# A fused attention and feed-forward kernel on one core: gate peaks taken from signed integers, all gate integers formed on ScalarE, forty of 48 gate units finished in the up pass and ten kept on chip

## The chip, the cores and the metric

The kernel runs on one core of a Trainium2 chip. The metric is device time of one execution in microseconds, as the median of several executions.

## The reference

Only the second half of the reference is touched by the change. With `x` of 8192 tokens by 512, and weights of 512 by 1536, it is

```python
def act_qdq(x):                      # 16 bits, one scale for the whole tensor
    scale = jnp.maximum(jnp.max(jnp.abs(x)) / qmax, 1e-12)
    return jnp.clip(jnp.round(x / scale), -qmax - 1.0, qmax) * scale

x = act_qdq(layernorm(x))
up = act_qdq(x @ lpbq_dequant(w_up).T)
gate = act_qdq(x @ lpbq_dequant(w_gate).T)
sig = fixed_qdq_u16(jax.nn.sigmoid(gate))     # round to 1/65536
gate = act_qdq(gate * sig)
o = act_qdq(gate * up)
return o @ lpbq_dequant(w_down).T             # added to the residual
```

Each `act_qdq` needs the largest magnitude of a whole tensor before its first integer can be formed. So there are four points at which everything waits for a peak: after `gate`, after `gate * sig`, after `up`, and after `gate * up`.

## The kernel before

The tokens are cut into 16 blocks of 512, and the 1536 columns into three parts of 512. One block by one part is a unit, 128 partitions by 2048 elements; there are 48 of each of `gate`, `up` and the product. After an attention part (the first 620 us), `feed` runs four stages.

**Gate pass.** TensorE makes the 48 gate units (L1778), each as two pairs of 1024 columns in four PSUM buffers. ScalarE copies each pair out (`evict`, L1640), VectorE takes the largest magnitude of the unit (`raw_peak`, L1421), and GpSimd's queue stores the raw float unit to DRAM. The raw unit sits in one of three buffers. Between these, the up and down weights are quantised: VectorE forms values (L1448, L1450), ScalarE their high halves (L1650).

**Up pass.** TensorE makes the 48 up units in the same way. Beside it, the other engines work on `gate`, in the order of a loop over the 48 tiles `n`. `first(u)` comes seven times in four tiles, from tile 0 to 26: the raw unit is loaded back into one of four buffers `gin`, made into 16-bit integers in a ring of four (on ScalarE, L1662, for every third unit, on VectorE, L1493, for the others) and stored; ScalarE also forms the magnitude of the integers in `ab` (L1664) and the sigmoid (L1666); VectorE rounds the sigmoid to an integer (`sigmoid_integer`, L1498) and multiplies magnitude and sigmoid with a running maximum (L1505). After all 48 the peak of `gate * sig` is known, and `second(v)`, two per tile from tile `SECOND` on, finishes `READY` units: sigmoid again (L1674), rounded (L1498), multiplied and scaled to the integers of the gated value (L1511), which go to DRAM and, for the first `KEPT` units, also stay in SBUF. For 13 of them (`DONE`: the kept ones and five late ones) ScalarE takes the magnitude in place right there (`magnitude`, L1682).

**Between the passes.** TensorE has nothing to do until the peak of `gate * up` is known. A loop over the 48 units, in an order made up beforehand, multiplies the magnitude of the gated integers with the magnitude of the up integers on VectorE, with a running maximum (`prod`, L1576). ScalarE forms the up magnitudes (`ua`, L1721) from raw up units that are loaded again; seven buffers hold them, so that a load is issued when the unit seven places before it is used. The gated integers are loaded by GpSimd's queue up to seven places ahead (`NEAR`), into `WQ` slots and into those of resident units that are used up. How a unit's gated magnitude comes about is its `made`:

- `done`: the magnitude is there, nothing is left to do
- `act`: ScalarE takes it (L1725)
- `dve`: VectorE takes it (L1567 and L1569)
- `late`: the unit was not finished in the up pass. ScalarE forms the sigmoid (L1708), VectorE rounds it (L1498) and multiplies (L1560), ScalarE scales and takes the magnitude (L1728)

The late units are spread evenly over the loop. With 36 finished units, the 48 are 12 late, 13 done, 15 act and 8 dve.

**Down pass.** With the peak known, the product's integers are formed unit by unit and TensorE multiplies them with the down weights (L1792).

Each engine runs its own list in order, with semaphores between them.

Of the kernel before, what the change touches and what calls it, by code (L numbers as in the profile page):

```python
# [6 lines left out]
F32 = mybir.dt.float32  # L7
F16 = mybir.dt.float16
I16 = mybir.dt.int16
U16 = mybir.dt.uint16  # L10
# [24 lines left out]
UN = 4  # L35
UNITS = FC // UN
UE = UN * BLK
READY = 36
EARLY = 4
XR = 9  # L40
KEPT = 8


def need(eng, sem, value):
# [868 lines left out]
def feed_memory(s, keep):  # L913

    for n, shape in (("up", [P, 2, DC, F]), ("down", [P, 2, FC, D])):
        keep[n + "_all"] = s.sb(n, shape, F16)
        keep[n] = [keep[n + "_all"][:, i] for i in range(2)]
    mem = {"gin": s.sb("gin", [P, 4, UE], F32), "ring": s.sb("ring", [P, 4, UE], I16),
           "sig": s.sb("sig", [P, 3, UE], F32), "sq": s.sb("sq", [P, UE], U16),
           "ab": s.sb("ab", [P, 2, UE], I16), "hq": s.sb("hq", [P, 2, DC * BLK], I16),  # L920
           "h_parts": s.sb("h_parts", [P, 2, 2, SUB, DC, P], F16), "raw": s.sb("raw", [P, UNITS, UE], F32)}
    for n in ("red_w", "all_w", "unit_w", *(f"{a}_{b}" for a in "gpuo" for b in ("red", "all"))):
        mem[n] = s.sb(n, [P, 1], F32)
    return mem


def feed(nc, keep, mem, hT_d, hq_d, gate_d, up_d, gate_q, x1_d, out, NB, scale_d, mats):
# [16 lines left out]
    SECOND = NU - READY // 2  # L944
    DONE = list(range(KEPT)) + [v for v in range(KEPT, READY) if v - KEPT >= AGAIN - AR][:5]
    LOADED = AGAIN - AR
    WQ, NEAR = 4, 7
    FG, FU = 4, 3
    hT_v = hT_d.rearrange("(b n) p d -> b p n d", n=SUB)
    out_v = out.rearrange("(b n p) d -> b p n d", p=P, n=SUB)  # L950
# [51 lines left out]
    with Scope(nc, "fd") as s:  # L1002
# [14 lines left out]
        def floats(t):  # L1017
# [23 lines left out]
                  for n in ("gate_all", "up_all"))  # L1041
# [16 lines left out]
        x_in, y_out = [s.sem(f"x_in{i}") for i in range(2)], [s.sem(f"y_out{i}") for i in range(2)]  # L1058
        m = s.sems("g_red g_all p_red p_all u_red u_all o_red o_all dve g_scales u_scales o_scales "
                   "hq ah al mm out peak w_peak w_red w_all w_scales w_sent w_q w_real w_hi w_lo "  # L1060
                   "gq_act gq_dve ab sig sq gpeak g2 mag gp neg ga_late ga_act ga_dve ua prod "
                   "fsig fsq fgp fgq fuq fo foq foh fol fmm y")
        gpk, gpk_v, gpk_p = whole_peak(nc, mem, m, "g", keep["gate_peak"][:, :])
        ppk, ppk_v, ppk_p = whole_peak(nc, mem, m, "p", keep["gated_peak"][:, :])
        upk, upk_v, upk_p = whole_peak(nc, mem, m, "u", keep["up_peak"][:, :])
        opk, opk_v, opk_p = whole_peak(nc, mem, m, "o", keep["o_peak"][:, :])
# [21 lines left out]

        def kept(j):

            return spare[:, j, :] if j < 6 else more[:, j - 6, :]

        def integers(u):

# [12 lines left out]

        def have_gq(eng, u):

            if u % 3 == 0:  # L1110
                eng.wait_ge(m["gq_act"], u // 3 + 1)
            else:
                eng.wait_ge(m["gq_dve"], u - u // 3)

        def gq_free(eng, u):

            if QR <= u < AWAY:
                eng.wait_ge(gq_out[u % QR], 16 * (u // QR))
                eng.wait_ge(m["sig"], u - QR + 1)

        def sig_free(eng, k):

# [17 lines left out]
        def gated(i):  # L1140

            kind, j = g_slot[i][0] if home[i] == "load" else ("unit", order[i])
            if kind == "wq":
                return hq[:, j, :] if j < 2 else ab[:, j - 2, :]
            return again(j - AWAY if j >= AWAY else j + KEPT)

        def have_gated(eng, i):
# [34 lines left out]
        with nc.Block() as block:  # L1182
            @block.sync
            def _(sp):
# [30 lines left out]
                def load_gate(u):  # L1215
                    if u < NU:
                        if u < GR:
                            sp.wait_ge(m["w_lo"], 2 * PIECES)
                            sp.wait_ge(m["hq"], NB)
                            sp.wait_ge(stored[u % UNITS], 16 * (u // UNITS + 1))  # L1220
                        else:
                            have_gq(sp, u - GR)
                            sp.wait_ge(m["ab"], u - GR + 1)
                            sp.wait_ge(stored[u % UNITS], 16 * (u // UNITS + 1))
                        sp.dma_start(gin[:, u % GR, :], gate_d[u // UNITS, u % UNITS]).then_inc(gate_in[u % GR], 16)

                def load_again(w):
                    if w < AGAIN:
                        if w < AR:
                            sp.wait_ge(m["sig"], NU)  # L1230
                            sp.wait_ge(m["ab"], NU)
                            for r in range(QR):
                                sp.wait_ge(gq_out[r], 16 * stored_first(r))
                        else:
                            sp.wait_ge(again_out[w % AR], 16 * (w // AR))
                        sp.dma_start(again(KEPT + w), gate_q[w]).then_inc(again_in[w % AR], 16)
# [90 lines left out]
            def _(pool):  # L1327
# [34 lines left out]
                for n in range(NU):  # L1362
# [5 lines left out]
                    if k == 1:  # L1368
                        pool.wait_ge(m["w_red"], i + 1)
                        nc.gpsimd.partition_all_reduce(allm[:, :], red[:, :], P, PEAK).then_inc(m["w_all"], 1)  # L1370
                gpk_p(pool)
                for n in range(NU):
                    if n == SECOND:
                        ppk_p(pool)
# [29 lines left out]
            def _(dve):  # L1404
# [13 lines left out]
                def raw_peak(n):  # L1418
                    dve.wait_ge(m["out"], 2 * n + 2)
                    to, k = ("gate_peak", n) if n < NU else ("up_peak", n - NU)  # L1420
                    nc.vector.tensor_reduce(keep[to][:, k:k + 1], raw[:, n % UNITS, :], AX.X, ALU.max,  # L1421
                                            apply_absolute_value=True).then_inc(m["peak"], 1)

# [52 lines left out]
                            weight_low(i, k // 2 - 3)  # L1476

                dve.wait_ge(m["peak"], NU)
                gpk_v(dve)
                link(nc.vector.tensor_tensor(g[:, 3:4], g[:, 0:1], al_[:, 5:6], ALU.mult))  # L1480
                dve.wait_ge(m["g_all"], 1)
                quantiser(nc, link, g[:, 4:5], g[:, 5:6], gpk[:, :], g[:, 2:3])
                nc.vector.tensor_scalar(g[:, 6:7], g[:, 4:5], 1.0 / 65536.0, None, ALU.mult).then_inc(m["g_scales"], 1)
                dve.wait_ge(m["g_scales"], 1)
                dve.wait_ge(m["w_lo"], 2 * PIECES)

                def gate_integers(u):
                    if 0 <= u < NU and u % 3:
                        dve.wait_ge(gate_in[u % GR], 16 * (u // GR + 1))
                        gq_free(dve, u)  # L1490
                        if u >= AWAY:
                            dve.wait_ge(m["mm"], NB * PAIRS)
                        nc.vector.tensor_scalar(integers(u), gin[:, u % GR, :], g[:, 5:6], None, ALU.mult).then_inc(m["gq_dve"], 1)  # L1493

                def sigmoid_integer(k, a):
                    dve.wait_ge(m["sig"], k + 1)
# [3 lines left out]

                def first(u):
                    sigmoid_integer(u, u % 2)
                    gate_integers(u + 2)
                    dve.wait_ge(m["ab"], u + 1)
                    nc.vector.tensor_tensor_reduce(out=sig[:, u % 2, :], in0=ab[:, u % 2, :], in1=sq[:, :], scale=1.0,  # L1505
                                                   scalar=0.0, op0=ALU.mult, op1=ALU.max,
                                                   accum_out=keep["gated_peak"][:, u:u + 1]).then_inc(m["gpeak"], 1)

# [2 lines left out]
                    nc.vector.scalar_tensor_tensor(out=again(v), in0=sq[:, :], scalar=g[:, 7:8], in1=again(v),  # L1511
                                                   op0=ALU.mult, op1=ALU.mult).then_inc(m["g2"], 1)

                gate_integers(1)
                for n in range(NU):
                    if n % UNITS == 1 and n // UNITS + 1 < NB:
                        split(NB + n // UNITS + 1)
                    for u in first_units(n):
                        first(u)
                    if n == SECOND - 1:  # L1520
                        dve.wait_ge(m["gpeak"], NU)
                        ppk_v(dve)
                    if n == SECOND:
                        dve.wait_ge(m["p_all"], 1)
                        quantiser(nc, link, g[:, 8:9], g[:, 7:8], ppk[:, :], g[:, 6:7])
                    for v in second_units(n)[:1]:
                        second(v)
                    raw_peak(NU + n)
                    for v in second_units(n)[1:]:
                        second(v)  # L1530
# [97 lines left out]
            def _(act):  # L1628
# [24 lines left out]
                    evict(n, 0)  # L1653
                    evict(n, 1)

                def first(u):
                    act.wait_ge(gate_in[u % GR], 16 * (u // GR + 1))
                    if u % 3 == 0:
                        gq_free(act, u)
                        if u >= AWAY:  # L1660
                            act.wait_ge(m["mm"], NB * PAIRS)
                        nc.scalar.activation(integers(u), gin[:, u % GR, :], ACT.Copy, scale=g[:, 5:6]).then_inc(m["gq_act"], 1)  # L1662
                    need(act, m["gpeak"], u - 1)
                    nc.scalar.activation(ab[:, u % 2, :], gin[:, u % GR, :], ACT.Abs, scale=g[:, 5:6]).then_inc(m["ab"], 1)  # L1664
                    have_gq(act, u)
                    nc.scalar.activation(sig[:, u % 2, :], integers(u), ACT.Sigmoid, scale=g[:, 4:5]).then_inc(m["sig"], 1)  # L1666

# [16 lines left out]
                act.wait_ge(m["g_scales"], 1)  # L1684
                act.wait_ge(m["w_lo"], 2 * PIECES)
                act.wait_ge(m["hq"], NB)
                for n in range(NU):
                    for u in first_units(n)[:1]:
                        first(u)
                    for v in second_units(n)[:1]:  # L1690
# [107 lines left out]
def build(nc, x, ctx_t, idx_t, wq_t, wkv_t, wo_t, gate_n, up_n, up_t, down_n, down_t, out, B, LKV):  # L1798
# [13 lines left out]
    with Scope(nc, "kept") as s:  # L1812
# [2 lines left out]

            "g": s.sb("g", [P, 16], F32),
            "h_peak": s.sb("h_peak", [P, NT // 2], F32), "gate_peak": s.sb("gate_peak", [P, U3], F32),
            "up_peak": s.sb("up_peak", [P, U3], F32), "gated_peak": s.sb("gated_peak", [P, U3], F32),
            "o_peak": s.sb("o_peak", [P, U3], F32),
        }  # L1820
        with Scope(nc, "kept") as s_gate:
# [62 lines left out]
```

## Time and profile before

| | us |
|---|---|
| median of 3 runs (2324.28 to 2326.08) | 2325.39 |
| the profiled execution | 2322.58 |
| its span, first to last instruction | 2320.7 |

The rows below are of the profiled execution; times are microseconds from the start of its span. PE is TensorE, DVE VectorE, ACT ScalarE, POOL GpSimd, SP the queue of loads. L1576 is line 1576 of the kernel before.

### The profile page before, as it was taken

To read this page: it belongs to the slowest core of one execution; us is meant where nothing else is said; L and a number is where in the kernel's file an instruction comes from. 1 tells how busy PE (TensorE), PEld (TensorE's weight loads), DVE (VectorE), ACT (ScalarE), POOL (GpSimd) and SP (SyncE) were. 2 spreads that over 40 slices of the span, in tenths; PEclk is the share of its full clock that TensorE was granted. 3 is DMA by queue.
4 is the path that set the end of the run, shared out by engine and by line. 5 is a ranking of instruction groups with operands and counts; after the bars stand their busy time and mean duration, and the time that the engine had idled before them with its cause. 6 is when DMAs were issued, how large, how long until landed. Compare 5 with 4: busy or idle time off the path is not lost.

```text
span 2320.7 us, 25770 instructions
## 1 busy us (share of the span) xinstructions
PE 2031.3 (88%) x9780; PEld 975.5 (42%) x9780; DVE 1678.2 (72%) x1385; ACT 1401.9 (60%) x1599; POOL 578.9 (25%) x600
## 2 busy tenths in 40 slices
PE   5899999998699999999999999998000799999998
PEld 2455555554344444444444444444000344444443
DVE  8799999999444443532699997999899644488641
ACT  4588888886322322322698995666899643467530
POOL 2587777776100000000112111222110000000000
PEclk9999999999799999999999999999555899999999
DMA  7689999997348647633899994787998755545641
GB/s 294 261 312 364 361 366 364 355 371 300 136 167 267 258 164 230 223 144 141 299 393 382 376 363 176 295 322 288 414 417 328 284 227 216 205 195 218 236 154 73
DMA packets 131163, 634.63 MB, mean 273 GB/s; under 512 B 12256, under 2 KB 12768, under 8 KB 91104
## 3 DMA queue, kind: packets, MB, share of 16 engines
q1 hardware_dynamic: 85888, 316.81, 37.3%
q0 software_dynamic: 45152, 316.16, 34.8%
q8 instruction: 78, 1.28, 0.2%
q14 instruction: 45, 0.37, 0.0%
HBM read 430.69 MB, written 202.24 MB: 273 GB/s over the span
## 4 chain that ended last, share of the span: by engine, by line
PE 64%; DVE 3%; issue 3%; ACT 2%; POOL 0%; DVEq 0%; ACTq 0%; POOLq 0%
PE fd_pp L1778 43%; PE fd_pp L1792 21%; ACT ff_ring L1721 1%; DVE ff_sig L1576 1%; DVE ff_h_parts L1560 1%; DVE ff_sq L1498 1%; ACT ff_sig L1708 0%; DVE ff_sq L1567 0%; DVE kept_gate L1569 0%; DVE ff_gin L1511 0%; DVE ff_hq L1550 0%; ACT ff_ring L1747 0%; ACT ff_sig L1737 0%; ACT ff_hq L1633 0%; DVE kept_o_peak L1576 0%
## 5 line engine op out<-in xcount | busy, mean ns | idle before, releaser
L1792 PE MATMUL fd_pp<-ff_down,kept_gate 128*128 128x512 f16 x1536 | 457.9, 380 | 193.1 <-DVE ff_up L1617 193.1
L1778 PE MATMUL fd_pp<-ff_h_parts,kept_gate 128*128 128x512 f16 x2304 | 500.4, 381 | 14.7 <-DVE ff_h_parts L1416 14.7
L1778 PE MATMUL fd_pp<-ff_h_parts,ff_up 128*128 128x512 f16 x2304 | 497.4, 379 | 0.0
L1640 ACT ACTIVATE ff_raw<-fd_pp 128x1024 f32<-128x1024 f32 x192 | 194.3, 1017 | 397.4 <-PE fd_pp L1778 397.4
L1778 PEld LDWEIGHTS fd_pp<-ff_h_parts,kept_gate 128*128 128x128 f16 x2304 | 226.1, 98 | 288.8 <-DVE ff_h_parts L1416 15.0
L1778 PEld LDWEIGHTS fd_pp<-ff_h_parts,ff_up 128*128 128x128 f16 x2304 | 225.4, 98 | 271.8
L1421 DVE TENSOR_REDUCE kept_gate_peak<-ff_raw 128x1 f32<-128x2048 f32 x48 | 109.7, 2285 | 293.5 <-ACT ff_raw L1640 293.5
L1792 PEld LDWEIGHTS fd_pp<-ff_down,kept_gate 128*128 128x128 f16 x1536 | 150.4, 98 | 375.2 <-issue 194.7
L1792 PE MATMUL fd_pp<-ff_down,ff_up 128*128 128x512 f16 x768 | 291.6, 380 | 0.0
L1747 ACT ACTIVATE ff_ring<-ff_hq,kept_g 128x2048 int16<-128x2048 f32 x48 | 96.0, 1999 | 189.5 <-DVE ff_hq L1550 188.2
L787 PE MATMUL at_psO<-kept_wo,at_ahi 128*128 128x512 f16 x512 | 154.9, 384 | 15.9 <-ACT at_alo L278 10.1
L1615 DVE CAST kept_gate<-ff_ring 128x2048 f16<-128x2048 int16 x48 | 33.3, 693 | 178.5 <-PE fd_pp L1792 135.1
L787 PE MATMUL at_psQ<-kept_wq,at_xhi 128*128 128x512 f16 x512 | 156.2, 387 | 1.4 <-ACT at_xlo L269 1.4
L518 DVE TENSOR_TENSOR at_kv_rows<-at_kv_rows,at_psQ 128x2048 f32<-128x2048 f32 x64 | 144.2, 2280 | 9.0 <-DMA at_kv_rows<-kv_table,kept_rows 5.0
L696 POOL TENSOR_TENSOR at_kv_rows<-at_kv_rows 128x1024 f32<-128x1024 f32 x62 | 146.7, 2367 | 4.9
L523 DVE TENSOR_REDUCE at_sc<-at_kv_rows 128x64 f32<-128x2048 f32 x64 | 142.9, 2274 | 0.0
L689 POOL TENSOR_TENSOR at_kv_rows<-at_kv_rows,at_pr 128x1024 f32<-128x1024 f32 x64 | 123.5, 1930 | 78.0 <-DVE at_kv_rows L528 74.2
L1335 POOL DMA_DIRECT2D gate_scratch<-ff_raw x48 | 26.5, 553 | 464.1 <-DVE kept_gate_peak L1421 464.1
L1395 POOL DMA_DIRECT2D out<-ff_h_parts x15 | 12.5, 834 | 466.0 <-DVE ff_h_parts L1593 439.0
L1498 DVE TENSOR_SCALAR ff_sq<-ff_sig 128x2048 uint16<-128x2048 f32 x96 | 117.3, 1222 | 9.5 <-ACT ff_sig L1666 6.0
L1421 DVE TENSOR_REDUCE kept_up_peak<-ff_raw 128x1 f32<-128x2048 f32 x48 | 109.5, 2282 | 18.5 <-ACT ff_raw L1640 18.2
L1792 PEld LDWEIGHTS fd_pp<-ff_down,ff_up 128*128 128x128 f16 x768 | 75.3, 98 | 91.1 <-issue 0.8
(239 smaller groups left out, 3311.8 us busy)
## 6 DMA issues: line engine op xcount, KB each, us to landing
ff_raw<-up_scratch SPq DMA_DIRECT2D x66, 1024.0 KB, 8.5
gate_scratch<-ff_raw POOLq DMA_DIRECT2D x48, 1024.0 KB, 9.1
ff_gin<-gate_scratch SPq DMA_DIRECT2D x48, 1024.0 KB, 8.4
up_scratch<-ff_raw POOLq DMA_DIRECT2D x48, 1024.0 KB, 6.8
ff_gin<-gate_integers SPq DMA_DIRECT2D x73, 512.0 KB, 6.3
gate_integers<-ff_ring POOLq DMA_DIRECT2D x43, 512.0 KB, 8.7
ff_up<-up_scratch SPq DMA_DIRECT2D x21, 1024.0 KB, 9.1
kept_xs<-in_x SPq DMA_DIRECT2D x32, 512.0 KB, 12.3
```

The source lines that it names most:

```text
L518: nc.vector.tensor_tensor(keys, keys, psQ[t % 2][:, :].unsqueeze(1).to_broadcast([P, W, D]), ALU.mult).then_inc(m["prod"], 1)
L523: nc.vector.tensor_reduce(raw[:, t % 2], kv[:, t % KR, :, 0:D].rearrange("p w (h e) -> p w h e", h=H), AX.X, ALU.add).then_inc(m["raw"], 1)
L689: nc.gpsimd.tensor_tensor(upper, upper, pr[:, t % 2, 2:4].unsqueeze(3).to_broadcast([P, 2, H, HD]), ALU.mult).then_inc(m["last"], 1)
L696: nc.gpsimd.tensor_tensor(lower, lower, upper, ALU.add).then_inc(m["half"], 1)
L787: mm = nc.tensor.matmul(out[:, :], a[:, slot, c, :], w[b][:, c, :], start=(q == 0), stop=(q == len(todo) - 1))
L1421: nc.vector.tensor_reduce(keep[to][:, k:k + 1], raw[:, n % UNITS, :], AX.X, ALU.max, apply_absolute_value=True).then_inc(m["peak"], 1)
L1498: nc.vector.tensor_scalar(sq[:, :], sig[:, a, :], 65536.0, 65535.0, ALU.mult, ALU.min).then_inc(m["sq"], 1)
L1615: nc.vector.tensor_copy(piece(oh, k), fo_oq).then_inc(m["foh"], 1)
L1640: nc.scalar.activation(raw[:, n % UNITS, h * 2 * BLK:(h + 1) * 2 * BLK], pp[(2 * n + h) % 4][:, :, :].rearrange("p a t -> p (a t)"), ACT.C ...
L1747: nc.scalar.activation(fo_oq, fo_o, ACT.Copy, scale=g[:, 13:14]).then_inc(m["foq"], 1)
L1778: mm = nc.tensor.matmul(pp[k % 4][:, h, :], wt[w][:, c, f:f + P], a[:, b % 2, :, c, :], start=(q == 0), stop=(q == len(todo) - 1))
L1792: mm = nc.tensor.matmul(pp[k % 8 // 2][:, k % 2, :], a[b % 2][:, f, t * P:(t + 1) * P], wt[w][:, f, :], start=(q == 0 and i == 0), stop=(q ...
```

## The change

The product's peak is now made from the signed gate integers: their product with the sigmoid, times -1, gives the largest negative one, and the largest positive one is worked out from the largest gate value alone (a second reduction, without magnitude, per unit of the gate pass), since the gated value grows with a positive gate. The magnitudes in `ab` are gone, and its two buffers keep two more finished units; ScalarE forms the integers of all 48 units, one unit ahead of its sigmoid. `READY` goes from 36 to 40, so that `SECOND` goes from tile 30 to 28, `KEPT` from 8 to 10, and `WQ` from 4 to 2.

```diff
-READY = 36
+READY = 40
...
-KEPT = 8
+KEPT = 10
...
-    WQ, NEAR = 4, 7
+    WQ, NEAR = 2, 7
...
-            return spare[:, j, :] if j < 6 else more[:, j - 6, :]
+            return spare[:, j, :] if j < 6 else more[:, j - 6, :] if j < 8 else ab[:, j - 8, :]
...
-            if u % 3 == 0:
-                eng.wait_ge(m["gq_act"], u // 3 + 1)
-            else:
-                eng.wait_ge(m["gq_dve"], u - u // 3)
+            eng.wait_ge(m["gq"], u + 1)
...
             if QR <= u < AWAY:
                 eng.wait_ge(gq_out[u % QR], 16 * (u // QR))
-                eng.wait_ge(m["sig"], u - QR + 1)
+                eng.wait_ge(m["gpeak"], u - QR + 1)
...
                             have_gq(sp, u - GR)
-                            sp.wait_ge(m["ab"], u - GR + 1)
...
-                gpk_p(pool)
+                pool.wait_ge(m["g_red"], 1)
+                nc.gpsimd.partition_all_reduce(g_all[:, :], g_red[:, :], P, PEAK).then_inc(m["g_all"], 1)
...
+                    if n < NU:
+                        nc.vector.tensor_reduce(keep["gate_top"][:, n:n + 1], raw[:, n % UNITS, :], AX.X, ALU.max)
                     nc.vector.tensor_reduce(keep[to][:, k:k + 1], raw[:, n % UNITS, :], AX.X, ALU.max,
                                             apply_absolute_value=True).then_inc(m["peak"], 1)
...
-                gpk_v(dve)
+                nc.vector.tensor_reduce(g_red[:, 0:1], keep["gate_peak"][:, :], AX.X, ALU.max)
+                nc.vector.tensor_reduce(g_red[:, 1:2], keep["gate_top"][:, :], AX.X, ALU.max).then_inc(m["g_red"], 1)
...
+                nc.vector.tensor_scalar(top_i[:, :], g_all[:, 1:2], g[:, 5:6], None, ALU.mult).then_inc(m["top"], 1)
+
+                def greatest_gated():
+                    dve.wait_ge(m["top_s"], 1)
+                    nc.vector.tensor_scalar(top_q[:, :], top_s[:, :], 65536.0, 65535.0, ALU.mult, ALU.min).then_inc(m["top_q"], 1)
+                    dve.wait_ge(m["top_q"], 1)
+                    link(nc.vector.tensor_tensor(keep["gated_peak"][:, NU:NU + 1], top_i[:, :], top_q[:, :], ALU.mult))
...
                 def first(u):
                     sigmoid_integer(u, u % 2)
-                    gate_integers(u + 2)
-                    dve.wait_ge(m["ab"], u + 1)
-                    nc.vector.tensor_tensor_reduce(out=sig[:, u % 2, :], in0=ab[:, u % 2, :], in1=sq[:, :], scale=1.0,
+                    nc.vector.tensor_tensor_reduce(out=sig[:, u % 2, :], in0=integers(u), in1=sq[:, :], scale=-1.0,
...
+                    if n == 2:
+                        greatest_gated()
...
-                def first(u):
-                    act.wait_ge(gate_in[u % GR], 16 * (u // GR + 1))
-                    if u % 3 == 0:
+                def gate_integers(u):
+                    if u < NU:
+                        act.wait_ge(gate_in[u % GR], 16 * (u // GR + 1))
                         gq_free(act, u)
                         if u >= AWAY:
                             act.wait_ge(m["mm"], NB * PAIRS)
-                        nc.scalar.activation(integers(u), gin[:, u % GR, :], ACT.Copy, scale=g[:, 5:6]).then_inc(m["gq_act"], 1)
+                        nc.scalar.activation(integers(u), gin[:, u % GR, :], ACT.Copy, scale=g[:, 5:6]).then_inc(m["gq"], 1)
+
+                def first(u):
+                    gate_integers(u + 1)
                     need(act, m["gpeak"], u - 1)
-                    nc.scalar.activation(ab[:, u % 2, :], gin[:, u % GR, :], ACT.Abs, scale=g[:, 5:6]).then_inc(m["ab"], 1)
                     have_gq(act, u)
                     nc.scalar.activation(sig[:, u % 2, :], integers(u), ACT.Sigmoid, scale=g[:, 4:5]).then_inc(m["sig"], 1)
...
+                gate_integers(0)
                 for n in range(NU):
+                    if n == 1:
+                        act.wait_ge(m["top"], 1)
+                        nc.scalar.activation(top_s[:, :], top_i[:, :], ACT.Sigmoid, scale=g[:, 4:5]).then_inc(m["top_s"], 1)
```

## Rows read from the trace of the kernel before

**Rows 1.** TensorE's waits: what waited for what, us in total, times, longest.

```profile
PE fd_pp L1792 <- DVE ff_up L1617: 193.1, 1, 193.1
```

**Rows 2.** Stretches: length, busy us of five engines, clock, DMA share, GB/s.

```profile
620.00:1120.80 500.80, 499.97 (x2303) 226.06 (x2304) 196.13 (x120) 135.06 (x118) 34.52 (x64) 0.99 0.58 203
1120.80:1618.50 497.70, 497.67 (x2306) 225.44 (x2304) 464.27 (x336) 395.39 (x256) 97.24 (x126) 1.00 0.84 321
...
1627.50:1802.10 174.60, 0.00 (x0) 0.00 (x0) 163.30 (x138) 162.77 (x86) 17.38 (x28) 0.50 0.94 384
1640.00:1740.00 100.00, 0.00 (x0) 0.00 (x0) 95.04 (x79) 96.27 (x52) 10.81 (x18) 0.50 1.02 419
1121.00:1411.00 290.00, 290.00 (x1345) 131.52 (x1344) 277.50 (x224) 265.55 (x168) 51.16 (x68) 1.00 0.91 349
```

**Rows 3.** Timeline between the passes: start, length, engine, line, operation, idle before.

```profile
1623.08 2.00 ACT L1708 ACTIVATE ff_sig<-ff_hq,kept_g 128x2048 f32<-128x2048 int16 x1
...
1627.59 5.79 ACT L1721 ACTIVATE ff_ring<-ff_raw,kept_g 128x2048 int16<-128x2048 f32 x3 [2.51 <-DVE kept_g L1536]
...
1781.82 1.89 ACT L1725 ACTIVATE ff_ab<-ff_ab 128x2048 int16<-128x2048 int16 x1
...
1783.62 1.99 ACT L1708 ACTIVATE ff_sig<-ff_sig,kept_g 128x2048 f32<-128x2048 int16 x1
...
1785.51 1.98 ACT L1721 ACTIVATE ff_ring<-ff_raw,kept_g 128x2048 int16<-128x2048 f32 x1
...
1789.75 1.22 DVE L1498 TENSOR_SCALAR ff_sq<-ff_sig 128x2048 uint16<-128x2048 f32 x1
...
1791.00 2.29 DVE L1560 TENSOR_TENSOR ff_h_parts<-ff_sig,ff_sq 128x2048 f32<-128x2048 int16 x1
1793.33 2.00 ACT L1728 ACTIVATE ff_sig<-ff_h_parts,kept_g 128x2048 int16<-128x2048 f32 x1 [0.25 <-DVE ff_h_parts L1560]
1793.43 0.69 DVE L1567 TENSOR_SCALAR ff_sq<-ff_gin 128x2048 int16<-128x2048 int16 x1
...
1795.30 2.29 DVE L1576 CUSTOM_DVE_ANT_0 ff_sig<-kept_gate,ff_ring 128x2048 bf16<-128x2048 int16 x1
...
1797.51 2.29 DVE L1576 CUSTOM_DVE_ANT_0 ff_sig<-ff_gin,ff_ring 128x2048 bf16<-128x2048 int16 x1
...
1801.94 0.08 DVE L1576 DVE_READ_ACCUMULATOR2_ANT kept_o_peak<- 128x1 f32 x1
```

**Rows 4.** Waits of VectorE and ScalarE between the passes, the longest that repeat.

```profile
DVE ff_sig L1576 <- ACT ff_ring L1721: 9.9, 9, 2.2
...
ACT ff_hq L1728 <- DVE ff_h_parts L1560: 2.6, 3, 2.1
```

**Rows 5.** Loads issued from 1618, 1630 and 1720 us on: size, us to landing.

```profile
ff_hq<-gate_integers POOLq DMA_DIRECT2D x1, 512.0 KB, 12.1
...
ff_up<-up_scratch SPq DMA_DIRECT2D x2, 1024.0 KB, 12.4
...
ff_raw<-up_scratch SPq DMA_DIRECT2D x3, 1024.0 KB, 6.9
```

**Rows 6.** Groups of instructions of the up pass: count, busy us, mean ns.

```profile
L1493 DVE TENSOR_SCALAR ff_ring<-ff_gin,kept_g 128x2048 int16<-128x2048 f32 x26 | 33.4, 1286 | 0.9
...
L1662 ACT ACTIVATE ff_ring<-ff_gin,kept_g 128x2048 int16<-128x2048 f32 x14 | 27.9, 1994 | 4.6 <-DVE kept_g L1483 4.6
```

**Rows 7.** Timeline from the gate pass to the up pass.

```profile
1121.03 44.19 PE L1778 MATMUL fd_pp<-ff_h_parts,ff_up 128*128 128x512 f16 x204
...
1122.29 2.29 DVE L1421 TENSOR_REDUCE kept_gate_peak<-ff_raw 128x1 f32<-128x2048 f32 x1 [8.07 <-ACT ff_raw L1640]
...
1133.97 1.00 ACT L1640 ACTIVATE ff_raw<-fd_pp 128x1024 f32<-128x1024 f32 x1
```

**Rows 8.** The gate pass: a wait of ScalarE, and the stores with us to landing.

```profile
ACT ff_up L1650 <- DVE ff_ring L1450: 23.2, 4, 5.8
...
gate_scratch<-ff_raw POOLq DMA_DIRECT2D x47, 1024.0 KB, 9.1
```

More of the change, by code:

```diff
@@ L921, in feed_memory @@
            "h_parts": s.sb("h_parts", [P, 2, 2, SUB, DC, P], F16), "raw": s.sb("raw", [P, UNITS, UE], F32)}
-    for n in ("red_w", "all_w", "unit_w", *(f"{a}_{b}" for a in "gpuo" for b in ("red", "all"))):
+    for n in ("red_w", "all_w", "unit_w", *(f"{a}_{b}" for a in "puo" for b in ("red", "all"))):
         mem[n] = s.sb(n, [P, 1], F32)
+    for n in ("g_red", "g_all"):
+        mem[n] = s.sb(n, [P, 2], F32)
+    mem["top_i"], mem["top_s"], mem["top_q"] = (s.sb(n, [P, 1], dt) for n, dt in (("top_i", I16), ("top_s", F32), ("top_q", U16)))
     return mem
@@ L1060, in feed @@
                    "hq ah al mm out peak w_peak w_red w_all w_scales w_sent w_q w_real w_hi w_lo "
-                   "gq_act gq_dve ab sig sq gpeak g2 mag gp neg ga_late ga_act ga_dve ua prod "
+                   "gq sig sq gpeak top top_s top_q g2 mag gp neg ga_late ga_act ga_dve ua prod "
                    "fsig fsq fgp fgq fuq fo foq foh fol fmm y")
-        gpk, gpk_v, gpk_p = whole_peak(nc, mem, m, "g", keep["gate_peak"][:, :])
+        g_red, g_all, top_i, top_s, top_q = (mem[n] for n in ("g_red", "g_all", "top_i", "top_s", "top_q"))
         ppk, ppk_v, ppk_p = whole_peak(nc, mem, m, "p", keep["gated_peak"][:, :])
@@ L1143, in gated @@
             if kind == "wq":
-                return hq[:, j, :] if j < 2 else ab[:, j - 2, :]
+                return hq[:, j, :]
             return again(j - AWAY if j >= AWAY else j + KEPT)
@@ L1229, in load_again @@
                         if w < AR:
-                            sp.wait_ge(m["sig"], NU)
-                            sp.wait_ge(m["ab"], NU)
+                            sp.wait_ge(m["gq"], NU)
+                            sp.wait_ge(m["gpeak"], NU)
                             for r in range(QR):
@@ L1478, in _ @@
                 dve.wait_ge(m["peak"], NU)
-                gpk_v(dve)
+                nc.vector.tensor_reduce(g_red[:, 0:1], keep["gate_peak"][:, :], AX.X, ALU.max)
+                nc.vector.tensor_reduce(g_red[:, 1:2], keep["gate_top"][:, :], AX.X, ALU.max).then_inc(m["g_red"], 1)
                 link(nc.vector.tensor_tensor(g[:, 3:4], g[:, 0:1], al_[:, 5:6], ALU.mult))
                 dve.wait_ge(m["g_all"], 1)
-                quantiser(nc, link, g[:, 4:5], g[:, 5:6], gpk[:, :], g[:, 2:3])
+                quantiser(nc, link, g[:, 4:5], g[:, 5:6], g_all[:, 0:1], g[:, 2:3])
                 nc.vector.tensor_scalar(g[:, 6:7], g[:, 4:5], 1.0 / 65536.0, None, ALU.mult).then_inc(m["g_scales"], 1)
@@ L1485, in _ @@
                 dve.wait_ge(m["w_lo"], 2 * PIECES)
[L1487 to L1493, printed above, removed]
+                nc.vector.tensor_scalar(top_i[:, :], g_all[:, 1:2], g[:, 5:6], None, ALU.mult).then_inc(m["top"], 1)
[4 more added lines that the diff above has]
+                    link(nc.vector.tensor_tensor(keep["gated_peak"][:, NU:NU + 1], top_i[:, :], top_q[:, :], ALU.mult))
                 def sigmoid_integer(k, a):
@@ L1512, in second @@
                                                    op0=ALU.mult, op1=ALU.mult).then_inc(m["g2"], 1)
-                gate_integers(1)
                 for n in range(NU):
+                    if n == 2:
+                        greatest_gated()
                     if n % UNITS == 1 and n // UNITS + 1 < NB:
@@ L1817, in build @@
             "h_peak": s.sb("h_peak", [P, NT // 2], F32), "gate_peak": s.sb("gate_peak", [P, U3], F32),
-            "up_peak": s.sb("up_peak", [P, U3], F32), "gated_peak": s.sb("gated_peak", [P, U3], F32),
+            "up_peak": s.sb("up_peak", [P, U3], F32), "gated_peak": s.sb("gated_peak", [P, U3 + 1], F32),
+            "gate_top": s.sb("gate_top", [P, U3], F32),
             "o_peak": s.sb("o_peak", [P, U3], F32),
```

## The prediction

> **What bounds the kernel now.** I read TensorE's waits first, because three of the four stages are matrix products. After the start of the gate pass the list holds one entry: 193.1 us before the first product of the down pass [rows 1]. Nothing else in three passes of about 500 us makes TensorE wait. The stretches say the same: in the gate pass and in the up pass it is busy for all but one microsecond [rows 2]. So time can come from one place, the gap between the up pass and the down pass, and be lost in the gate and up passes, where the change lengthens other engines' lists.
>
> I then looked at what fills the gap. From the first up magnitude at 1627.59 to the last product's accumulator at 1801.94 plus 0.08 [rows 3] are 174.4 us, and in them VectorE is busy 163.30 and ScalarE 162.77 us [rows 2]: two engines share the bound, handing work to each other. What lies around these 174.4 us (the last matmul to the peak of up before, the chain over the last peak to the first product behind) is made of the same instructions in both kernels.
>
> Last I looked at the transfers, for a third bound as near: the DMA share is 1.02 at 419 GB/s from 1640 to 1740 us, and 0.94 over the whole gap [rows 2].
>
> **The gap, unit by unit.** Durations overlap at their ends, so I price an instruction by the step to the next start [rows 3]. Every unit costs ScalarE one up magnitude, 1.89 (5.79 for three in a row gives 1.90), and VectorE one product, 2.21 (1795.30 to 1797.51). A late unit adds on ScalarE 1.89 (sigmoid, 1783.62 to 1785.51) and 1.91 (its magnitude, 2.00 less the same overlap), 3.80 together; on VectorE 1.25 (1789.75 to 1791.00) and 2.21 (a 2.29 us operation less the overlap), 3.46 together. An act unit adds 1.80 on ScalarE (1781.82 to 1783.62), a dve unit 1.87 on VectorE (1793.43 to 1795.30), a done unit nothing.
>
> Going through the loop that makes the order by hand gives, with L late, d done, a act, v dve:
>
> Before: ddd, Ldad, Lvda, Ldad, Lvda, Ldad, Lvda, Ldav, four times Laav, L: 12 late, 13 done, 15 act, 8 dve.
>
> After: dddda, Ldvdad, Ladvda, Ldadvd, Ladadv, Ldaava, Lavaav, Laavaa, L: 8 late, 15 done, 17 act, 8 dve.
>
> The totals before are ScalarE 48 x 1.89 + 12 x 3.80 + 15 x 1.80 = 163.3 (161.4 without the first sigmoid, which runs at 1623.08 ahead of the stretch) and VectorE 48 x 2.21 + 12 x 3.46 + 8 x 1.87 = 162.6, against 162.77 and 163.30 measured [rows 2], so the prices hold to 1%. After, they are 151.7 and 148.8.
>
> Since the up magnitudes run only three ahead, the engines can't trade slack over long stretches. So I take for each group the greater demand. Before: 6.6 for ddd; 13.16 (ScalarE) for each of three Ldad; 14.17 (VectorE) for each of three Lvda and for Ldav; 14.96 (ScalarE) for each of four Laav; 5.7 for the last L; 168.3 together. The measured 174.4 is 6.1 more: 2.1 until the first magnitude is ready, and some 0.3 in each ScalarE group, where the engines wait for each other [rows 4]. After: 11.25, then 18.59 (VectorE), 18.74, 18.59, 18.74, 20.54, 20.54, 22.34 (ScalarE), and 5.7: 155.0, which is 13.3 less. I add 0.5 to the overhead: the first sigmoid belongs to the sixth unit now and no longer runs ahead of the stretch, and the first gated unit is wanted as the fifth unit's magnitude, at 1627.59 + 5 x 1.9 = 1637.1, while a load issued there landed 12.1 us after its issue [rows 5], about 1638.5; VectorE's rounding and product of the late unit cover most of that. **The gap shrinks by 12.8 us.**
>
> If the engines never waited for each other, ScalarE's 151.7 with 2.1 at the start and one product behind would take 156.0, 18.4 less than now. That is the bound above. For the one below see the loads.
>
> **The other parts.** *Gate pass.* 48 more reductions. The trace has no reduction without a magnitude; it may cost as little as the 0.69 of VectorE's quickest pass over a unit [rows 3], or as much as the 2.29 with one [rows 7]; I take 2.29, the same operation on the same tile. That is 106 us on VectorE at a step of 2.2, where it is busy 196.13 of 500.8 [rows 2]. What waits behind it is the store, and ScalarE for the weight pieces, now 5.8 us each (23.2 over four), then 8.0. A raw buffer is wanted again five pairs of 5.18 us (497.7 / 96) after its last copy, 25.9; reduction, store and landing take 2.3 + 0.3 + 9.1 [rows 8], then 2.2 more, which leaves 12. ScalarE late by 2.2 finds TensorE up to four pairs ahead. Cost nothing; with the cover gone, 2.2 per unit.
>
> *The seam.* The gate scale comes 2.5 us later (the second reduction of the last unit and three tiny operations). The first copy of the up pass stands behind three ScalarE operations in both versions; it ended at 1134.97 [rows 7], and TensorE needs its buffer for the fifth pair at 1120.8 + 4 x 5.18 = 1141.5. Of 6.5 us, 4.0 stay. Cost nothing. The one-column sigmoid and its integer lie between 0.08, the shortest one-column row [rows 3], and 1 us, once: nothing.
>
> *Up pass.* VectorE loses 32 gate integers (1.286 each [rows 6]) and gains four finished units of some 3.5: 464 becomes 438 of 497.7. ScalarE loses 48 magnitudes, gains 32 integers, four sigmoids and two more magnitudes in place: 395 becomes about 376. In the first 290 us, where both run fullest (277.5 and 265.6 [rows 2]), they fall to about 238 and 236. The product with scale -1 is taken at the 2.29 of the same operation in the gap [rows 3]; it could cost 40% more before VectorE were as full as now. Finishing starts at tile 28 instead of 30, and the firsts end in tile 26; with VectorE at 238 of 290 they no longer run behind their tiles, so the earlier start finds the peak known. The queues carry four more stores of finished units and two more loads of integers, and two stores of integers less, 0.524 MB each: 2.1 MB more beside the 160 of this pass (321 GB/s for 497.7 us), whose share is 0.84. TensorE was never held, so all this relief is worth nothing.
>
> The Trainium skill (ScalarE: Activation LUTs, Rules for kernel authors) advises against this move: multiplications belong on VectorE, up to about three times faster in bf16. Rows 6 agree in direction, with 1.286 against 1.994 us; the sum would be worse by that only if ScalarE were the bound of the up pass.
>
> *Down pass.* Four fewer late units are formed again, under TensorE's work: nothing. Its clock stands at 0.50, the 1.2 GHz level, in the gap while it idles [rows 2], and it starts from there either way.
>
> **The sum.** Against the profiled 2322.58 us: 2309.8. The median of the runs lies 2.8 above that execution, so I predict **2312.6**.
>
> **Rivals.** *The loads pace the gap.* 45 raw up units of 1.049 MB and 29 gated ones of 0.524 (31 less two that are loaded early) were 62.4 MB; after, 28 of the latter make it 61.9. If the stretch at share 1.02 can't shorten, it gives back 0.5 MB, 1.3 us at 419 GB/s; only the last third, where ScalarE's 16 units cost 59.8 and then 57.8, gives 2 more: **2322**. For it speaks the share. In the four groups of six that follow the first five units, 24 up and 14 gated loads are 32.5 MB, 77.6 us, against 74.7 of work. Against it speaks the time to landing, which falls from 12.4 to 6.9 us through the stage [rows 5]: the queue drains, and no engine waits for a load [rows 4]. It would now grow by some 3 us, to 15, where a load is issued seven units, 22 us, ahead.
>
> The Trainium skill (DMA: Bandwidth & Descriptors, Where 436 GB/s comes from) has a rule by which this rival would win outright: between HBM and SBUF the limit of about 358 GB/s per core binds. By it 61.9 MB take an estimated 173 us, and the gap could not shrink. Here the trace disagrees, with 419 GB/s held for 100 us.
>
> *ScalarE holds the up pass.* Each gate integer now waits in ScalarE's list, ahead of the PSUM copies, for its load and for the store of the unit four before. Seven units and eight copies need 7 x 3.8 + 8 x 1.0 = 34.6 of four tiles' 41.5 us, so 1.0 us of wait per unit is free. Beyond that TensorE falls behind; from 1.35 the gain is spent and 4.7 us more. At 2.0 per unit it costs 48: **2361**. Against it: four units are 23.7 us, and landing takes 9 to 12 [rows 5, 8]; every third unit waited so before, and TensorE did not.
>
> *The handovers eat half.* Groups of six cluster ScalarE's extra work; at 1 us of waits more per group the gain is 6: **2319**.
>
> **How the numbers follow.** The likeliest case, a gain of 10 to 16, has 0.76; handovers or loads in part, 5 to 10, have 0.10; more than 16 has 0.03; these are faster. The loads in full, or nothing for another reason, 0.06; a held up pass or gate pass, 0.05. About 0.2%, 4.7 us, is what a measurement can tell from no change. So faster 0.89, same 0.06, slower 0.05. The likeliest case alone is 2309.5 to 2315.5; the range goes from the engine bound, 2307.0, to near the handover case, 2318.5.
>
> **What would show it.** TensorE's wait ahead of the down pass at 180 instead of 193.1 us, and still no other after 621 us; eight late units; ScalarE at about 152 us of busy time there, VectorE at 149; a DMA share of 1.0 that lasts to the end of the loads, with landing at 11 to 15 us and no wait of the up magnitudes for a load. The prediction is wrong if those magnitudes wait for DMA, or if TensorE waits for a ScalarE copy in the up pass.

## The result, and the profile after

The changed kernel takes 2347.73 us in the median (2344.23 to 2350.41, 4 runs), against 2324.84 (2323.17 to 2326.08) for the kernel before: a ratio of 1.0098, interval 1.0081 to 1.0116. It is slower by 23 us, where 12.8 us of gain were forecast.

TensorE's waits, read first again, answer to [rows 1]:

```profile
PE fd_pp L1799 <- DVE ff_up L1618: 193.0, 1, 193.0
PE fd_pp L1785 <- DVE ff_h_parts L1416: 31.0, 4, 14.4
```

The wait ahead of the down pass is as long as before, and the second line is new in its count: one of its four is the 14.4 us at the start of the gate pass, which was there before too (14.73 us before the product at 620.83); the other three, 16.6 us together, lie in the up pass. L1416 is VectorE's `split` of a block's hidden integers (`hq`) into the two halves that TensorE multiplies. The chain of waits names what holds it (start, length, what; the lines of three of four such places):

```profile
1477.25 2.30 DVE kept_up_peak L1423
1480.78 5.01 DMA gate_integers<-ff_gin
1486.18 5.55 DMA ff_hq<-h_integers
...
1519.54 6.46 DMA gate_integers<-ff_gin
1526.38 4.47 DMA ff_hq<-h_integers
...
1558.68 6.17 DMA gate_integers<-ff_gin
1565.24 4.71 DMA ff_hq<-h_integers
```

A store of finished gate integers ends, and only then a load of `hq` starts. The timeline of the second place shows the engines (with the idle time before, and its releaser):

```profile
1519.54 0.53 POOL L1346 DMA_DIRECT2D gate_integers<-ff_gin  x1
...
1526.02 0.32 SPq L1235 DMA_DIRECT2D ff_gin<-gate_integers  x1
1526.38 0.54 SPq L1213 DMA_DIRECT2D ff_hq<-h_integers  x1
...
1530.88 0.69 DVE L1414 CAST ff_h_parts<-ff_hq 128x2048 f16<-128x2048 int16 x1 [9.06 <-DMA ff_hq<-h_integers]
...
1532.89 3.60 PE L1785 MATMUL fd_pp<-ff_h_parts,ff_up 128*128 128x512 f16 x9 [4.93 <-DVE ff_h_parts L1416]
...
1534.06 2.00 ACT L1677 ACTIVATE ff_sig<-ff_gin,kept_g 128x2048 f32<-128x2048 int16 x1 [9.82 <-DVE ff_sq L1500]
```

The order on SP's queue explains it. In tile `n`, SP issues the `hq` load of a coming block if the tile is the first of a block, and then two loads of gate integers, `w = 2 (n - SECOND)` and the next. A load goes into the slot of load `w - 9`, once that unit is finished and its store has landed; that is the unit finished as number `w - 9 + KEPT`. With 8 kept this is `w - 1`, so the tile's two loads wait for units of the tile before and of the same tile. With 10 kept it is `w + 1`, and the second load waits for a unit that VectorE finishes first in tile `n + 1`. The `hq` load of the tile after stands behind it, and VectorE's split, which needs `hq`, stands one tile further, ahead of everything else VectorE has to do there. So once per block VectorE finishes a unit, waits for its store, and then for the load: 9 us, four times. Its waits from 1410 to 1645 us:

```profile
DVE ff_h_parts L1414 <- DMA ff_hq<-h_integers: 36.3, 4, 9.6
```

In the kernel before, VectorE waits for `hq` once in the up pass, 4.7 us near its start, and never beside the finishing of units. Part of the delay comes from another queue: the unit stored at 1519.54 was finished 3.4 us earlier, at 1516.10, but GpSimd's queue issues the store of a raw up unit ahead of it, and that one waits for its peak. No run moved it.

The stretches behind the second, third and fourth place, and the gap (columns as in [rows 2]):

```profile
1533.00:1537.00 4.00, 4.00 (x12) 1.45 (x11) 3.96 (x3) 2.91 (x2) 0.00 (x0) 0.57 0.00 0
1537.00:1541.00 4.00, 4.00 (x20) 1.81 (x19) 3.96 (x3) 1.22 (x1) 1.48 (x2) 1.00 0.20 70
...
1572.00:1576.00 4.00, 4.00 (x10) 1.48 (x11) 3.96 (x3) 2.84 (x2) 0.00 (x0) 0.50 0.02 4
...
1611.60:1615.60 4.00, 3.98 (x11) 1.46 (x12) 3.96 (x3) 2.81 (x2) 0.00 (x0) 0.54 0.02 4
...
1660.70:1828.00 167.30, 0.00 (x0) 0.00 (x0) 149.53 (x128) 153.14 (x81) 15.98 (x27) 0.50 0.96 393
```

After a wait of 5 to 6 us the granted clock is near 0.5, the 1.2 GHz level, for about 4 us: 10 to 12 products start where 20 do later. From the first gate product to the last up product are 997.7 us before (620.83 to 1618.5) and 1020.5 after (624.20 to 1644.66): 16.6 of the 22.8 are waits, the remaining 6.2 go with the lower clock.

The gap itself shrank. Its first and last rows, which answer to those of [rows 3]:

```profile
1660.77 3.90 ACT L1728 ACTIVATE ff_ring<-ff_raw,kept_g 128x2048 int16<-128x2048 f32 x2 [7.44 <-DVE kept_g L1537]
...
1828.02 0.08 DVE L1577 DVE_READ_ACCUMULATOR2_ANT kept_o_peak<- 128x1 f32 x1
```

It starts 16.1 us after the last up product, where it was 9.1 (ScalarE and VectorE are behind by the last stall, as the first experiment shows), and lasts 167.3 us instead of 174.4. The waits of ScalarE and of VectorE in it, against [rows 4]:

```profile
ACT ff_sig L1715 <- DMA ff_sig<-gate_integers: 3.7, 1, 3.7
...
ACT ff_sig L1715 <- DMA kept_gate<-gate_integers: 1.2, 1, 1.2
ACT ff_sig L1715 <- DMA ff_ab<-gate_integers: 1.1, 1, 1.1
```

```profile
DVE ff_sig L1577 <- ACT ff_ring L1728: 17.0, 13, 3.0
```

ScalarE now waits 6.0 us for loads, which it never did before: all of them gated integers of late units, for their sigmoids.

The attention part differs by up to 5.0 us between profiled executions, and no edit touches it. From the first gate product to the end are 1699.9 us before and 1722.4 after, 22.5 more: 22.8 in the passes, 7.0 later start of the gap, 7.1 less gap, and 0.2 less behind it.

### The profile page after: what moved, and what is told of

The parts are those of the page before. It is cut to its first block, busy times and chain, and to the rows that moved or that the text cites. A ratio compares the mean times of both kernels' runs of the same rounds, so it can differ in the third digit from the quotient of the medians.

```text
span 2346.6 us, 25717 instructions
## 1 busy us (share of the span) xinstructions
PE 2038.6 (87%) x9780; PEld 977.7 (42%) x9780; DVE 1733.2 (74%) x1397; ACT 1358.5 (58%) x1576; POOL 570.8 (24%) x600
## 4 chain that ended last, share of the span: by engine, by line
PE 57%; DVE 6%; issue 4%; DMA 3%; ACT 2%; POOL 0%; SPq 0%; DVEq 0%; ACTq 0%; POOLq 0%
PE fd_pp L1785 36%; PE fd_pp L1799 21%; DVE ff_gin L1511 2%; DVE ff_sq L1500 2%; ACT ff_ring L1728 1%; DMA gate_integers<-ff_gin 1%; DMA ff_hq<-h_integers 1%; DMA ff_sig<-gate_integers 1%; DVE ff_h_parts L1561 0%; DVE kept_up_peak L1423 0%; DVE ff_sig L1577 0%; DMA ff_ab<-gate_integers 0%; DVE ff_ring L1511 0%; ACT ff_sig L1715 0%; ACT kept_gate L1732 0%
## 5 line engine op out<-in xcount | busy, mean ns | idle before, releaser
L1785 PE MATMUL fd_pp<-ff_h_parts,ff_up 128*128 128x512 f16 x2304 | 504.3, 382 | 16.6 <-DVE ff_h_parts L1416 16.6
L1785 PE MATMUL fd_pp<-ff_h_parts,kept_gate 128*128 128x512 f16 x2304 | 499.7, 380 | 14.4 <-DVE ff_h_parts L1416 14.4
L1422 DVE TENSOR_REDUCE kept_gate_top<-ff_raw 128x1 f32<-128x2048 f32 x48 | 109.7, 2286 | 190.2 <-ACT ff_raw L1641 190.2
L787 PE MATMUL at_psO<-kept_wo,at_ahi 128*128 128x512 f16 x512 | 155.5, 386 | 17.2 <-ACT at_alo L278 10.1
```

The source lines that it names most:

```text
L787: mm = nc.tensor.matmul(out[:, :], a[:, slot, c, :], w[b][:, c, :], start=(q == 0), stop=(q == len(todo) - 1))
L1422: nc.vector.tensor_reduce(keep["gate_top"][:, n:n + 1], raw[:, n % UNITS, :], AX.X, ALU.max)
L1785: mm = nc.tensor.matmul(pp[k % 4][:, h, :], wt[w][:, c, f:f + P], a[:, b % 2, :, c, :], start=(q == 0), stop=(q == len(todo) - 1))
```

## Experiments

Two causes were to be told apart for the up pass: the order on SP's queue, or ScalarE's and VectorE's lists themselves (all gate integers on ScalarE, finishing from tile 28). For the gap: late units' loads, or the handovers between the two engines. The ratios are to the kernel before as it ran beside each experiment: 2323.35 us in the median beside the first four, 2325.01 beside the last two. In the expectations, e1 to e6 are the experiments in this order.

**The hidden integers loaded two tiles earlier** (the changed kernel otherwise):

```diff
-                    if n % UNITS == 0:
-                        load_hq(n // UNITS + 1)
+                    if n == 0:
+                        load_hq(1)
+                    if n % UNITS == 1:
+                        load_hq(n // UNITS + 2)
```

> The changed kernel, with each load of a block's hidden integers (hq) put two tiles earlier in SP's queue. Theory 'queue order': in the changed kernel this load stands on SP's queue behind loads of gate integers that wait for a unit finished one tile later, VectorE's split waits for it, and everything behind VectorE with it; TensorE's three waits in the up pass (16.6 us), the clock lost behind them (about 7) and the later start of the gap (7) go, so 2348 - 31 = 2317 us, and the gap between 1661 and 1828 us keeps its 167 us. Rival 'ScalarE list': the integers and their waits in ScalarE's list, or the start at tile 28, hold the up pass, and the load is late only because everything is; then TensorE still waits 10 us or more there and the time stays at 2340 to 2350.

Measured: 2316.58 us (ratio to before 0.9973, 0.9963 to 0.9984). TensorE's waits and, from the gap, those of ScalarE for loads:

```profile
PE fd_pp L1801 <- DVE ff_up L1620: 186.5, 1, 186.5
...
PE fd_pp L1787 <- DVE ff_h_parts L1418: 14.3, 1, 14.3
```

```profile
ACT ff_sig L1717 <- DMA ff_sig<-gate_integers: 2.2, 2, 1.9
...
ACT ff_hq L1734 <- DMA ff_hq<-gate_integers: 2.0, 1, 2.0
...
ACT ff_sig L1717 <- DMA kept_gate<-gate_integers: 1.4, 1, 1.4
...
ACT ff_sig L1717 <- DMA ff_ab<-gate_integers: 1.2, 1, 1.2
```

All three waits in the up pass are gone, and 31 us by the medians with them (29.1 in the profiled executions, from the first gate product on), with ScalarE's and VectorE's lists as they were. The gap starts 9.1 us after the last up product again, and keeps 167.8 us, with 6.8 us of waits for loads.

**Eight units kept** (the changed kernel, SP's order untouched):

```diff
-KEPT = 10
+KEPT = 8
```

> The changed kernel with 8 units kept instead of 10 (still 40 finished, and two slots for gated units); the load order on SP's queue is untouched. With 8 kept, a load of gate integers waits for a unit that was finished two places earlier than with 10, one tile. Theory 'queue order': the waits of TensorE in the up pass go (0 to 3 us left), as without the change, and the time is 2315 to 2322. Rival 'ScalarE list': ScalarE's and VectorE's lists are nearly the same, so TensorE waits 10 us or more and the time stays at 2340 to 2350.

Measured: 2319.03 us (ratio 0.9980, 0.9971 to 0.9990).

```profile
PE fd_pp L1799 <- DVE ff_up L1618: 188.2, 1, 188.2
...
PE fd_pp L1785 <- DVE ff_h_parts L1416: 14.3, 1, 14.3
```

No wait in the up pass. It is the two more kept units that stall the queue, through the unit that a load waits for, and neither the forty finished ones nor the signed integers.

**The kernel before, with the load behind the tile's two loads:**

```diff
-                    if n % UNITS == 0:
-                        load_hq(n // UNITS + 1)
                     for u in first_units(n):
                         load_gate(u + GR)
                     if n >= SECOND:
                         sp.wait_ge(m["peak"], NU + n - 1)
                         load_again(2 * (n - SECOND))
                         load_again(2 * (n - SECOND) + 1)
+                    if n % UNITS == 0:
+                        load_hq(n // UNITS + 1)
```

> The kernel before, with one move: the load of the hidden integers stands behind the tile's two loads of gate integers on SP's queue instead of ahead of them. That puts it behind the same unit as in the changed kernel, for three blocks instead of four. Theory 'queue order': VectorE waits some 9 us three times at its split, TensorE waits 4 to 6 us twice or three times in the up pass, and the time grows by 15 to 25 us, to 2340 to 2350. Rival 'ScalarE list': a load of 0.5 MB three tiles ahead has room enough, nothing moves, 2325.

Measured: 2359.23 us (ratio 1.0155, 1.0134 to 1.0176). TensorE's waits from 1130 to 1660 us, and of these the ones up to 1410 and from 1520 on; then VectorE's from 1410 us on:

```profile
PE fd_pp L1778 <- DVE ff_h_parts L1416: 21.5, 6, 7.2
```

```profile
PE fd_pp L1778 <- DVE ff_h_parts L1416: 7.6, 4, 4.6
...
PE fd_pp L1778 <- DVE ff_h_parts L1416: 13.9, 2, 7.2
```

```profile
DVE ff_h_parts L1414 <- DMA ff_hq<-h_integers: 29.5, 3, 11.1
```

The stall of the changed kernel can be made in the kernel before, by order on the queue alone. It costs 36 us, where I expected 15 to 25. The part that I expected is there: three stalls of VectorE (29.5 us, the longest 11.1) and two waits of TensorE behind them (13.9). But the edit puts the load behind the loads of raw gate units in tiles 0 to 26 as well, which the expectation left out; there TensorE waits four times more, 7.6 us, which is no copy of anything in the changed kernel. With the lower clock behind these waits the gap starts 34 us later after the first gate product than before.

**The load early, and gated units up to ten places ahead:**

```diff
-    WQ, NEAR = 2, 7
+    WQ, NEAR = 2, 10
```

> As e1_hq_early, and gated units are loaded up to ten places ahead in the gap instead of seven. Theory 'late loads': the gap shrank by 7.2 instead of 12.8 us because ScalarE's sigmoids of late units, which come three places ahead, waited 6.0 us for their gated integers; with ten places these waits fall to 0 to 2 us, the gap to 162 or 163 us, and the time to 4 or 5 us below e1. Rival 'handovers': VectorE's waits for ScalarE (17.0 us in the changed kernel's gap, 9.9 before) come from the way the units' work clusters; then the gap stays at 166 to 168 and the time within 1.5 us of e1.

Measured: 2311.80 us (ratio 0.9955, 0.9938 to 0.9971). TensorE's wait, ScalarE's only wait for a load in the gap, and VectorE's:

```profile
PE fd_pp L1801 <- DVE ff_up L1620: 183.0, 1, 183.0
```

```profile
ACT ff_hq L1734 <- DMA ff_hq<-gate_integers: 1.9, 1, 1.9
```

```profile
DVE ff_sig L1579 <- ACT ff_ring L1730: 14.0, 10, 3.0
```

The gap as one stretch (columns as above):

```profile
1625.90:1790.20 164.30, 0.00 (x0) 0.00 (x0) 149.41 (x129) 152.75 (x81) 15.99 (x27) 0.50 0.98 404
```

The late units' loads no longer hold ScalarE. The time is 4.8 us below the first experiment's, within the 4 to 5 expected; the gap is 164.3 us, 3.5 less, where 162 or 163 was expected. VectorE still waits 14.0 us for ScalarE, so the late loads were worth 3.5 us of the gap, and the rest goes with handovers, which no run took away.

**The kernel before with 40 finished units alone:**

```diff
-READY = 36
+READY = 40
```

> The kernel before with 40 instead of 36 finished units and nothing else: magnitudes in ab, two thirds of the gate integers on VectorE, 8 kept, finishing from tile 28 instead of 30. Its loads wait for a unit two places earlier than in the changed kernel, so the queue does not stop. If taking work off VectorE in the first 290 us is worth nothing, as the prediction had it, the time is that of e2_kept8, 2319. Rival: VectorE, some 10 us behind its tiles when the firsts end, reaches tile 28 late and carries that to the end of the up pass; then the gap starts 3 to 8 us later, TensorE may wait a few us, and the time is 2322 to 2330.

Measured: 2320.22 us (ratio to before 0.9987, 0.9977 to 0.9997).

```profile
PE fd_pp L1792 <- DVE ff_up L1617: 190.5, 1, 190.5
...
PE fd_pp L1778 <- DVE ff_h_parts L1416: 14.2, 1, 14.2
```

```profile
ACT ff_sig L1737 <- DMA ff_raw<-up_scratch: 6.3, 1, 6.3
```

TensorE has no wait in the up pass, and the gap starts as early as with the signed integers (1005.5 us after the first gate product, 1005.9 in the first experiment) and lasts as long, 167.8 us. So VectorE's backlog does no harm, and the relief in the up pass is worth nothing, as the prediction had it. In this kernel the first up unit of the down pass is waited for, 6.3 us, where the first experiment waits 2.4 us for the last product. TensorE's wait ahead of the down pass is 4.0 us longer by it (190.5 against 186.5), and with that go the 3.3 us between them in the table below.

**Forty-two finished units, on top of the fourth experiment:**

```diff
-READY = 40
+READY = 42
```

> As e4_hq_early_near10, with 42 finished units: 6 late, 15 done, 18 act, 9 dve, finishing from tile 27. By the engine sums ScalarE falls from 151.7 to 145.9 and VectorE from 148.8 to 143.7, so the gap shrinks by 4 to 6 us, to 159 or 160, and the time by as much, to 2306 to 2308. Rival 'loads pace the gap': the bytes hardly change, so the up magnitudes or late sigmoids wait for loads and the gap stays at 163 to 165 us, the time at 2311 to 2313. A third outcome: with finishing from tile 27, right behind the last of the firsts, the up pass is held and the time is over 2315.

Measured: 2314.60 us (ratio to before 0.9953, 0.9935 to 0.9971), no different from the fourth. ScalarE's and VectorE's waits in the gap:

```profile
ACT ff_sig L1717 <- DMA ff_ab<-gate_integers: 5.6, 1, 5.6
ACT ff_hq L1734 <- DMA ff_hq<-gate_integers: 4.8, 1, 4.8
```

```profile
DVE ff_sig L1579 <- ACT ff_ring L1730: 21.3, 8, 12.8
```

The gap up to ScalarE's last instruction in it, the first 21 us of the gap, and the issue of the load behind the wait of 5.6 us:

```profile
1629.20:1792.40 163.20, 0.00 (x0) 0.00 (x0) 141.21 (x123) 146.73 (x78) 16.42 (x27) 0.50 0.98 402
...
1629.20:1650.00 20.80, 0.00 (x0) 0.00 (x0) 8.94 (x8) 10.44 (x6) 2.11 (x4) 0.50 1.01 419
...
1633.93 0.53 POOL L1359 DMA_DIRECT2D ff_ab<-gate_integers  x1 [4.83 <-DVE kept_o_peak L1579]
```

Both engines' busy times fall as the sums said: VectorE's over the whole gap to 144.10 us (143.7), ScalarE's for its 78 instructions to 146.73 (145.9). But the gap is 166.1 us, where 159 or 160 were expected. It is not the up magnitudes that wait. Two loads of gated integers at the start of the gap, one for the magnitude of an act unit and one for the sigmoid of a late one, hold ScalarE for 10.4 us, and VectorE behind it for 12.8 once. So the rival was right in kind: the loads take back what the engines gain, at one place. The late unit's load is issued at 1633.93, when the first product has freed its slot, and lands 15 us later, while the DMA share is 1.01. Whether the issue or the full transfers hold it, and whether another order of the first units would free it, no run tells.

All in one table; the last columns are of the profiled executions, from the first gate product on:

| kernel | median us | to the end | against before | gap |
|---|---|---|---|---|
| before | 2324.84 | 1699.9 | | 174.4 |
| changed | 2347.73 | 1722.4 | +22.5 | 167.3 |
| `hq` early | 2316.58 | 1693.3 | -6.6 | 167.8 |
| 8 kept | 2319.03 | 1693.8 | -6.1 | 169.4 |
| before, `hq` behind | 2359.23 | 1734.2 | +34.3 | 174.5 |
| `hq` early, ten ahead | 2311.80 | 1689.4 | -10.5 | 164.3 |
| before, 40 finished | 2320.22 | 1696.6 | -3.3 | 167.8 |
| the fourth, 42 finished | 2314.60 | 1689.3 | -10.6 | 166.1 |

## Why the prediction was wrong

**The step that failed** is the one on the queues in the up pass: "The queues carry four more stores of finished units and two more loads of integers, and two stores of integers less", weighed by bytes and found hidden. The bytes were hidden. The order was not looked at: that `KEPT` enters the choice of the unit for which a load waits, that this moved by two units, one tile, and that a load of another kind stands behind it on SP's queue. The first and second experiments remove the stall by the two ends of that chain, the third makes it in the kernel before. With the stall go 16.6 us of waits, 6.2 us at the lower clock, and 7 us by which the gap starts later.

**The rival on the other side** had the right place, the up pass, and the wrong mechanism. ScalarE's gate integers do not hold anything: with the same lists, the first experiment's TensorE has no wait. What held TensorE was VectorE's split, and not a copy of ScalarE, as that rival had it. To go against the rule of the Trainium skill that speaks for VectorE (ScalarE: Activation LUTs, Rules for kernel authors) cost nothing here.

**Gate pass, seam, relief, down pass** were priced at nothing, and are: no wait of TensorE from the first gate product up to 1527 us in the changed kernel, and none in the up pass of five of the six others. What lies behind the gap takes 518.7 us before and 518.5 after. The second reduction, for which there was no row, takes the 2.29 us assumed; in the first 290 us of the up pass VectorE and ScalarE are busy 249.79 and 239.11 us, for about 238 and 236.

**The gap** was mis-sized: 7.1 us instead of 12.8. Its engine sums were right, 153.14 and 149.53 busy us for 151.7 and 148.8. The overhead was put at 6.6 us and is 12.3 (167.3 against 155.0). I had taken every load to be seven places ahead of its use. That holds for up units; the sigmoid of a late unit comes three places ahead of the unit, so its gated integers have four. And ScalarE runs ahead of the products, by which places are counted. The load that was waited for longest, and the sigmoid behind it:

```profile
1676.75 8.91 DMA ff_sig<-gate_integers
```

```profile
1685.69 2.00 ACT L1715 ACTIVATE ff_sig<-ff_sig,kept_g 128x2048 f32<-128x2048 int16 x1 [3.72 <-DMA ff_sig<-gate_integers]
```

ScalarE was ready at 1681.97, 5.2 us after the issue, and the load took 8.9. With ten places 3.5 us come back. The rest, 2.7 us, I put down to handovers, which I had let shrink with the late units; that is argued, since no run takes them away.

**The loads as a bound** were a rival at 6%, by which the gap could give 3.3 us. At 40 finished units the runs are against it: the gap gave 7.1 us, and 10.1 in the fourth experiment, where no up magnitude waits for a load though the share is 0.98. At 42 the loads of two gated units do hold the gap, at a share of 1.01. The rule of the Trainium skill that about 358 GB/s bind (DMA: Bandwidth & Descriptors, Where 436 GB/s comes from) is contradicted again: 404 GB/s over the 164.3 us of the fourth experiment's gap.

With two points of order mended the change takes 2311.80 us, 0.45% less than before. That gain is not shown to be the signed integers' or the two kept units': forty finished units alone take 2320.22 us with a gap of 167.8, as long as the first experiment's. Whether ten places would serve that kernel as well was not run.

## What to carry to other kernels

When a change alters a count that enters an index, work out for every wait on a ring slot which earlier piece of work it now waits for, and in which tile that is finished. Then look at what else stands behind that wait on the same queue: a small load of another kind there can hold an engine that has nothing to do with the ring. And price a prefetch by the distance from its issue to its first use, not by the number of buffers.

## What the hardware showed that I had not expected

A wait of TensorE of 5 to 6 us costs more than itself: the granted clock was 0.57, 0.50 and 0.54 in the 4 us after the three waits, and three waits of 16.6 us in sum lengthened the two passes by 22.8. In the third experiment it was 0.50, 0.59 and 0.50 in the 4 us after waits of 4.6, 6.6 and 7.3 us, and 1.00 after one of 1.9.
